# Gate and up projection of layer 2 moved ahead of the late scores in the first two head pairs

## The reference

```python
xn = layernorm(x)
# attention: 16 query heads of 64 features, one shared key and value head, causal
q = layernorm(xn)*g1 @ Wq.T ; k, v = split(layernorm(xn)*g1 @ Wkv.T)
q, k = 4 * q/|q|, 4 * k/|k|
out = softmax(causal(q @ k.T)) @ v
attn = layernorm(out @ Wout.T) * g2
# feed-forward: 384 hidden features
gate, up = xn @ w_gate.T, xn @ w_up.T
ffn = (silu(gate) * up) @ w_down.T
x = x + attn + ffn
```

## Time and profile before

| | |
|---|---|
| median of 3 runs | 1593.21 us (1591.64 to 1596.76) |
| profiled execution | 1599.2 us, span 1597.4 us |
| granted TensorE clock, mean | 0.938 |
| PE busy | 1315.1 us (82%) |
| DVE busy | 965.2 us (60%) |
| ACT busy | 693.7 us (43%) |
| POOL busy | 484.6 us (30%) |

### The profile page before, as it was taken

The page is one execution under the profiler, slowest core; times in us unless marked ns, Lnnn a source line. Parts: engine busy times, 40 slices in busy tenths (PEclk is TensorE's granted clock), DMA queues, the critical chain, the costliest instruction groups (busy, mean ns, idle before and its releaser), DMA issues. The chain is left out here.

```text
span 1597.4 us, 29359 instructions
## 1 busy us (share of the span) xinstructions
PE 1315.1 (82%) x8780; PEld 865.9 (54%) x8780; DVE 965.2 (60%) x2535; ACT 693.7 (43%) x1069; POOL 484.6 (30%) x820
## 2 busy tenths in 40 slices
PE   3787878787887878875996598998989898989897
PEld 1544444444444444434996366665665656565664
DVE  4676767676766767646442456565665656575644
ACT  1353545454544545441442252526353444445351
POOL 2121212121212112116331252525343434434241
PEclk9899989888898999896998699999999999999998
DMA  2200000000000000006111000000000000000000
GB/s 67 61 19 9 13 14 14 8 20 7 13 14 14 14 14 13 14 1 188 46 46 30 1 8 1 13 0 13 0 13 0 13 0 10 3 7 7 7 1 7
DMA packets 35266, 29.63 MB, mean 19 GB/s; under 512 B 6656, under 2 KB 27776, under 8 KB 35200
## 3 DMA queue, kind: packets, MB, share of 16 engines
q1 hardware_dynamic: 32416, 24.22, 5.5%
q0 software_dynamic: 2304, 4.72, 1.3%
q10 hardware_dynamic: 480, 0.00, 0.0%
HBM read 13.72 MB, written 6.82 MB: 13 GB/s over the span
## 5 line engine op out<-in xcount | busy, mean ns | idle before, releaser
L1377 DVE CUSTOM_DVE_ANT_0 dump<-ring_d,masks 128x512 bf16<-128x512 f32 (+1 forms) x512 | 307.4, 623 | 157.4 <-PE ring_d L349 126.2
L1127 ACT ACTIVATE arena<-ring_a 128x896 f32<-128x896 f32 x256 | 228.2, 917 | 205.1 <-PE ring_a L349 193.3
L349 PE MATMUL ring_d<-rows,q_rows 128*128 128x512 f32 (+1 forms) x512 | 243.7, 511 | 74.3 <-DVE mx L1377 62.9
L900 POOL TENSOR_SCALAR_AFFINE_SELECT arena<-arena 128x256 f32<-128x256 f32 x256 | 119.8, 468 | 539.5 <-ACT arena L1127 539.5
L1251 ACT ACTIVATE arena<-ring_a 128x896 f32<-128x896 f32 (+1 forms) x192 | 163.3, 885 | 204.7 <-PE ring_a L349 204.6
L349 PEld LDWEIGHTS ring_d<-rows,q_rows 128*128 128x128 f32 x512 | 104.6, 212 | 217.5 <-DVE mx L1377 160.3
L349 PE MATMUL ring_a<-rows,k_rows 64*128 64x512 f32 (+3 forms) x1536 | 158.5, 339 | 43.9 <-ACT xn_all L1231 26.4
L349 PEld LDWEIGHTS ring_a<-rows,k_rows 64*128 64x128 f32 x1536 | 119.8, 190 | 81.1 <-ACT xn_all L1231 29.4
L1018 POOL TENSOR_TENSOR q_len<-q_sum,exponents 128x8 f32<-128x8 f32 x64 | 105.3, 1645 | 178.9 <-DVE q_sum L1675 178.9
L349 PE MATMUL ring_a<-q_max,rows 128*128 128x384 f32 (+1 forms) x512 | 158.7, 394 | 1.0 <-ACT arena L1127 0.6
L349 PE MATMUL ring_d<-arena,v_aug 128*64 128x512 f32 (+3 forms) x1024 | 150.2, 438 | 0.0
(11 more groups left out here) (212 smaller groups left out, 1996.5 us busy)
## 6 DMA issues: line engine op xcount, KB each, us to landing
rows<-k_rows SPq DMA_DIRECT2D x128, 64.0 KB, 2.0
arena<-in_w SPq DMA_DIRECT2D x2, 2048.0 KB, 15.1
slots_y<-arena SPq DMA_DIRECT2D x40, 64.0 KB
x_all<-in_x SPq DMA_DIRECT2D x8, 256.0 KB, 4.0
tokens_x<-xn_all SPq DMA_DIRECT2D x1, 2048.0 KB, 9.5
out<-o_t SPq DMA_DIRECT2D x8, 256.0 KB, 2.3
arena<-tokens_x,tokens_now POOLq DMA_INDIRECT x40, 2.6
wq_sb<-in_wq_t SPq DMA_DIRECT2D x1, 512.0 KB, 5.5
```

The source lines that it names most:

```text
L349: return pe.matmul(out, lhs, rhs, start=start, stop=stop, skip_group_check=True)
L900: pool.affine_select(out=v, in_=v, compare_op=ALU.is_ge, fill=0.0, base=0, pattern=[[0, 2], [-1 if half == 0 else 1, P]], channel_multipli ...
L1127: act.activation(probs[:, h % 8, half * HALF0:(half + 1) * HALF0], sl[:, 128:1024] if half == 0 else sl[:, 0:HALF0], ACT.Exp).then_inc(A.f ...
L1377: dve.tensor_tensor_reduce(dump[:, h % 2, 0:many], D.slot(("max", g, i, h))[:, 0:many], masks[:, m, at:at + many], 1.0, LOWEST, ALU.add, A ...
```

## The change

In pairs 0 and 1 `gate_up(n + 1)` moves, on PE and on ACT. On PE it stood behind `turn_q(n + 1)` and now stands between `project_q(n + 2)` and `late_scores(n)`. On ACT it stood behind `q_turned(n + 1)` and now stands between the second and third exponential. `squares(n + 2)` of these two pairs moves from there to the end of the pair, and on DVE `q_sums` moves behind `q_low(n + 1)`. No instruction is added or taken away, and POOL's program is the same.

```diff
@@ PE
                     scores(n)
                     if n + 2 < NP:
                         project_q(n + 2)
+                    if n < 2:
+                        gate_up(n + 1)
                     late_scores(n)
                     if n + 1 < NP:
                         turn_q(n + 1)
-                    if n < 2:
-                        gate_up(n + 1)
                     if n:
                         values1(n - 1)
@@ ACT
                     exp_of(n, 0)
                     exp_of(n, 1)
-                    if n + 2 < NP:
+                    if n < 2:
+                        gate_up(n + 1)
+                    elif n + 2 < NP:
                         squares(n + 2)
                     exp_of(n, 2)
                     if n + 1 < NP:
                         q_turned(n + 1)
                     if n < 2:
-                        gate_up(n + 1)
+                        squares(n + 2)
@@ DVE
                 for n in range(NP):
-                    if n + 2 < NP:
+                    if n > 1 and n + 2 < NP:
                         q_sums(s, n + 1, b)
                     if n + 1 < NP:
                         dve.wait_ge(A.free.sem, A.emptied(b, ("q.T", n + 1)))
                         q_low(n + 1)
+                    if n < 2:
+                        q_sums(s, n + 1, b)
                     if n + 2 < NP:
                         q_unit(s, n + 2, b)
```

## The result

The kernel after took 1620.5 us (median, 1614.7 to 1620.85) where the kernel before took 1594.73 us beside it (1591.64 to 1596.76). The ratio is 1.0155, with 95% between 1.0125 and 1.0185: **slower by 25.8 us**. The forecast was 1614.0 us, 20.8 us slower, in a range of 1603 to 1626. So side and range held, and the cost came out some 5 us above the sum. The profiled execution of the kernel after took 1620.66 us, its span 1618.9 us.

What follows compares the result with a forecast made beforehand. PE's work plus its holes up to scores(3) was taken to bound each batch. Terms of 0.62, 1.72 and 0.25 us made 2.6 a batch, +20.8 over eight batches: 1593.2 + 20.8 = 1614.0 us, range 1603 to 1626.

Steps and rivals of the forecast that it cites:

- What bounds the batch: PE up to scores(3): its work plus its holes set the time; holes grow from 2.6 to about 5.2 us.
- Pair 0: turn_q(1) on PE waits for ACT to empty the chunk's slot: hole of 0.9 us, scores(1) 0.62 us later.
- Pair 1: ACT's tanh of chunk 2 waits for silu_up(0): hole of 2.3 us ahead of turn_q(2), +1.72 us.
- Pair 2: On PE, turn_q(3) waits for the late q_unit(3): +0.25 us.
- Sum: Over pairs 0 to 2: 0.62 + 1.72 + 0.25 = 2.6 us a batch, +20.8 us in eight batches.
- Clock: PE's clock falls behind pair 0's new holes in most batches, nearly free; net nothing, +8 us kept for the range.
- one of the clock: Rival: on PE, a clock fall with nothing to cover it in each batch; +8 us, 1622; chance 0.14.
- The quick root chain: Rival: root chain quicker by 1.4 us, turn_q(2) waits only for the chunk; +10 us, 1603; chance 0.08.
- the late DVE: Rival: DVE's queue still late at pair 3, turn_q(4) and turn_q(5) wait; some 1 us a batch, 1622; chance 0.06.
- The case without loss: Rival: turn_q(1) starts right behind the late scores, scores(1) as before; -4 us, 1589; not slower or within bound 0.06.

Runs made afterwards that it cites:

- held clock: Kernel after with PE repeating unread matmuls in its holes, 1611.21 us, against the kernel before with its holes filled likewise, 1592.78 us.
- pair 0 alone: New order in pair 0 only, old order in pair 1, against the kernel before: 1619.33 us, 1.0133; with holes filled 1600.36 us, 1.0010.
- the early silu_up: Kernel after with silu_up(0) and silu_up(1) at the start of their pairs on DVE: 1618.65 us, 1.0137 to before; with holes filled 1602.33 us.
- the squares in their old place: Kernel after with squares on ACT and q_sums on DVE moved back: 1619.33 us, 1.0147 to before; with holes filled 1603.22 us, 1.0032.
- pair 1 alone: New order in pair 1 only, old order in pair 0, against the kernel before: 1604.87 us, 1.0046.

## Why the prediction was right, step by step

- **What bounds the batch** (PE's work plus the holes up to scores(3)): right. 61.4 us from scores(3) on in both kernels, holes 2.6 to 5.0 us (forecast 5.2), batch +2.45 (forecast 2.6).
- **Pair 0**, scores(1) at 8.01: measured 8.18, +0.80 for the forecast +0.62. The hole ahead of turn_q(1) was 0.76 for 0.9. What was too small is the last link: PE starts 0.23 us behind the end of q_low (1448.35 to 1448.58), where I had 0.05, the link behind ACT's copy. The chunk's place was told too narrowly: by the prediction's own numbers the slot delays the copies by 0.19 (1171.53 to 1171.72), and the rest is ACT's order, which puts the chunk ahead of them.
- **Pair 1**, silu_up(0) as the last to come: right by name; by size the pair added 1.42 us for 1.72. POOL's root 8.63 (8.75), hole 1.94 (2.3), values1(0) 15.23 (15.35), scores(2) 17.53 (17.66). The late scores(1) didn't add to it, since the wait hides it, and the two pairs together added 2.22 for 2.34.
- **Pair 2**, +0.25 for turn_q(3): it waited 0.16, and the pair grew by 0.23.
- **Sum**: 8 x 2.6 = 20.8; 18.4 at held clock. The steps were put 2.4 us too high and the clock too low, and part of the nearness of the forecast is that these two offset each other.
- **Clock**: the step that failed. I took its net at nothing, with falls behind pair 0's holes covered and others behind the hole of 2.3 us. The first half held (+0.28 in the third batch, where pair 0 alone and the early silu_up, without cover, mostly lost 1.25 to 1.4). But the second batch had a longer one that cost 1.5, and the falls that cost most came at scores(0), behind the old hole of 1.68 us, which the change doesn't touch: in three of six batches, 1.24 to 1.28 us each. With the four covered falls of 0.3 to 0.35 us that is 6.5 us in the profiled span; by the medians it is 25.8 - 18.4 = 7.4 us, with some 5 us of uncertainty.
- **Rivals**: one of the clock named this mechanism, and its price (+8 us, 1622) was closer to the time than the forecast. A fall with no cover in *each* batch is somewhat more than was seen, four in the six batches from the second on that cost their full price (the second, third, fourth and sixth). The quick root chain, the late DVE and the case without loss did not occur. The case without loss was also argued wrongly: had turn_q(1) started right behind the late scores, ACT would still have had the chunk and the third exponential ahead of the copies, and scores(1) would have come some 0.4 us late by the prediction's own numbers (0.62 less the 0.19 of the slot).

The prediction weighed the Trainium skill's "TensorE: Matmul & The Clock Gate", section "A second HAM failure mode: psum-queue depth-cycling", by which frequent short idle times between groups of matmuls make the clock go back and forth. By that rule the change costs more than its holes. The trace agrees: 21.2 us in the six batches where the steps make 14.7. Filling the holes of after, with no change in the order, brought 0.8% (1.0155 to 1.0075).

Why the old hole at scores(0) led to a fall in four of eight batches after (first, third, fourth, sixth) and in two before (first, last) isn't settled. The work ahead of it is the same instructions at the same distances. Each kernel has one trace, so the counts are rough: a fall at scores(0) came in four batches of pair 0 alone, four of the early silu_up, five of the squares in their old place, and two of pair 1 alone. What differs is when a batch starts; that the alignment to something in the chip decides is a guess, and no run tested it.

## What to carry to other kernels

In a ring with two slots, ask of a moved step not only whether its own result is late, but who gets its slot next, what chain hangs behind that one, and what its emptying stands ahead of in the other engine's order. Here a chunk moved ahead of the late scores put ACT's 1.5 us ahead of a chain of 2.8 us (transposes, copies, q_low). Follow a second move's effects through the first: two moves of 0.8 and 0.6 us together made a wait of 1.1 that neither has alone. Where the clock falls behind short holes, compare steps with the holes filled on both sides; without that, of two causes that cover each other, either looks worth next to nothing.

## What the runs showed of the hardware

Two short holes close together, 0.77 and 2.15 us, were followed by a fall to 1.2 GHz in the third batch of pair 0 alone, and every batch of it took over 1 us more than with the holes filled. The same two holes were followed by none in the seventh batch of after. One hole of 1.68 us gave a fall in some batches and none in others of the same kernel. A fall cost 1.2 to 1.4 us in most cases where nothing covered it, and up to 2.5 us (second batch of pair 0 alone, 10.42 us from scores(1) to scores(2), for 7.94 with the holes filled). Repeated matmuls in the holes kept the granted clock at 1.00 from 990 to 1580 us in every kernel that had them.

q_low on DVE lasted 0.96 us beside POOL's masks and 0.69 without them. The Trainium skill says in "SBUF — State Buffer", section "Who interferes with whom", that DVE and GpSimd share a pair of ports to SBUF and that the one holding it shuts the other out. This row agrees: the masks had started first (1174.16) and took their usual 1.49 us, and q_low, started at 1175.22, took 0.27 us longer. That it was the ports is by that page; no run here tests it.

PE started 0.23 us after the end of q_low (1448.35 to 1448.58), but 0.06 us after the end of another DVE instruction, q_unit (1255.27 to 1255.33), and 0.05 us after that of ACT's copy (1172.94 to 1172.99). Such links belong in the sum with a size of their own, read from a row with the same pair of steps.
